# Windowed attention in a fused transformer kernel: probabilities turned on VectorE in 32x32 blocks and placed by DMA instead of turned on TensorE

## The reference, cut to what matters

```
h = layernorm(layernorm(x)) ; qkv = h @ qkv_w + qkv_b         # 16 heads of 16
scores = einsum('bld,blwd->blw', q, kw) / 4                   # each token sees 15 neighbours
attn = softmax(scores, axis=-1)
out = einsum('bld', attn, vw) ; x = x + (shortcut + out @ proj_w + proj_b, then gelu MLP 256-1024-256)
main = gelu(x @ W1m + b1m) @ W2m + b2m
top_vals, top_idx = top_k(softmax(mean(x) @ w_gate + b_gate), 2)
out = x + a * main + (1 - a) * sum_k gate_k * (gelu(x @ W1e[k] + b1e[k]) @ W2e[k] + b2e[k])
```

## Time and profile before

| | |
|---|---|
| Median of 3 runs | 1894.2 us (1894.03 to 1895.52) |
| Profiled execution: span | 1891.2 us |
| PE busy | 1877.7 us (99%) |
| DVE busy | 1348.4 us (71%) |
| ACT busy | 1173.0 us (62%) |
| POOL busy | 875.4 us (46%) |
| DMA | 121.88 MB, mean 64 GB/s |

### The profile page before, as it was taken

The page is one execution under the profiler, slowest core; times in us unless marked ns, Lnnn a source line. Parts: engine busy times, 40 slices in busy tenths (PEclk is TensorE's granted clock), DMA queues, the critical chain, the costliest instruction groups (busy, mean ns, idle before and its releaser), DMA issues.

```text
span 1891.2 us, 49280 instructions
## 1 busy us (share of the span) xinstructions
PE 1877.7 (99%) x19591; PEld 1684.3 (89%) x19591; DVE 1348.4 (71%) x2230; ACT 1173.0 (62%) x1832; POOL 875.4 (46%) x788
## 2 busy tenths in 40 slices
PE   8999999999999999999999999999999999999999
PEld 6889898898988989889898888988889898898998
DVE  7776877777677686776767767677776777777644
ACT  5775755657566575665756657566575655657554
POOL 6555271542715436153362524536245271552725
PEclk9999999999999999999999999999999999999999
DMA  4220312203122031210313113131131311203121
GB/s 141 67 86 28 96 57 54 71 29 96 57 70 64 20 102 51 83 58 24 96 45 90 51 31 94 40 96 47 41 89 34 96 57 48 77 29 96 46 62 57
DMA packets 147437, 121.88 MB, mean 64 GB/s; under 512 B 17964, under 2 KB 140040, under 8 KB 147208
## 3 DMA queue, kind: packets, MB, share of 16 engines
q1 hardware_dynamic: 146512, 117.90, 21.7%
q10 hardware_dynamic: 696, 0.83, 0.2%
HBM read 85.52 MB, written 8.39 MB: 50 GB/s over the span
## 4 chain that ended last, share of the span: by engine, by line
PE 97%; DVE 1%; ACT 0%; DMA 0%; issue 0%; POOL 0%; ACTq 0%; DVEq 0%; POOLq 0%
PE psB L253 58%; PE psA L253 28%; PE psA L1258 3%; PE psA L1275 3%; PE psA L1297 2%; PE psA L1147 2%; PE psA L1313 0%; DMA raw<-in_L_attn_qkv_w 0%; DVE smax L733 0%; POOL wf_lo L501 0%; DVE smax L720 0%; DVE pr L737 0%; DVE hr_lo L622 0%; PE psB L1332 0%; DMA xin<-in_L_attn_x 0%
## 5 line engine op out<-in xcount | busy, mean ns | idle before, releaser
L622 DVE TENSOR_TENSOR hr_lo<-hf,hr_hi 128x512 fp32r<-128x512 f32 x512 | 484.0, 945 | 467.4 <-ACT hr_hi L976 467.4
L510 POOL TENSOR_SCALAR wx_hi<-raw 128x512 fp32r<-128x512 f32 x256 | 201.6, 788 | 668.6 <-DMA raw<-in_L_ffn_W2e 390.4
L976 ACT ACTIVATE hr_hi<-hf 128x512 fp32r<-128x512 f32 x512 | 324.4, 634 | 277.8 <-PE psB L253 189.7
L512 POOL TENSOR_TENSOR wx_lo<-raw,wx_hi 128x512 fp32r<-128x512 f32 x256 | 409.3, 1599 | 21.4
L253 PE MATMUL psB<-wx_hi,hr_hi 128*128 128x256 f32 x1016 | 287.6, 283 | 1.5 <-DVE acc L654 0.3
L972 ACT ACTIVATE hf<-psB,b1x 128x512 f32<-128x512 f32 x256 | 175.3, 685 | 176.1 <-PE psB L253 173.4
L253 PE MATMUL psB<-wx_hi,hr_lo 128*128 128x256 f32 x1016 | 284.2, 280 | 0.0
L253 PE MATMUL psB<-wx_lo,hr_hi 128*128 128x256 f32 x1016 | 283.6, 279 | 0.0
L253 PE MATMUL psB<-z_hi,wx_hi 128*128 128x512 f32 x512 | 212.1, 414 | 0.0
L253 PEld LDWEIGHTS psB<-wx_hi,hr_hi 128*128 128x128 f32 x1016 | 191.0, 188 | 19.6 <-issue 7.3
L253 PE MATMUL psB<-z_hi,wx_lo 128*128 128x512 f32 x512 | 202.4, 395 | 0.0
(11 more groups left out here) (207 smaller groups left out, 4644.0 us busy)
## 6 DMA issues: line engine op xcount, KB each, us to landing
raw<-in_L_ffn_W1e SPq DMA_DIRECT2D x256, 128.0 KB, 2.3
raw<-in_L_ffn_W2e SPq DMA_DIRECT2D x256, 128.0 KB, 2.2
vb<-vs SPq DMA_DIRECT2D x64, 192.0 KB
vb<-vs SPq DMA_DIRECT2D x64, 160.0 KB
out_x<-acc SPq DMA_DIRECT2D x31, 256.0 KB, 2.2
xin<-in_L_attn_x SPq DMA_DIRECT2D x15, 512.0 KB, 3.8
tm<-in_L_ffn_b2e SPq DMA_DIRECT2D x32, 128.0 KB, 3.3
raw<-in_L_attn_fc_w SPq DMA_DIRECT2D x8, 256.0 KB, 3.1
```

Of the source, the lines that this page charges most:

```text
L510: g.tensor_scalar(wx[0][:, s, :], raw[:, s, :], 1.0, 0.0, ALU.mult, ALU.add).then_inc(w_hi.sem, 1)
L512: g.tensor_tensor(wx[1][:, s, :], raw[:, s, :], wx[0][:, s, :].bitcast(f32), ALU.subtract).then_inc(w_lo.sem, 1)
L622: v.tensor_tensor(hr[1][:, c % 2, :], hf[:, c % 3, :], hr[0][:, c % 2, :].bitcast(f32), ALU.subtract).then_inc(h_lo.sem, 1)
L976: a.activation(hr[0][:, c % 2, :], hf[:, c % 3, :], ACT.Copy).then_inc(h_hi.sem, 1)
```

## The change

Row 0 stays nearly as it is (`turn_first`, `turned_first`). In rows 1 to 15:

- `turn` on PE and `turned` on ACT go. In their place DVE turns a unit in blocks of 32x32 with one instruction (`turn_blocks`), behind `normalise`: units 0 to 3 at q 3, 4, 8 and 9. The result goes into `y` (unit 0), the new tile `blk` (units 1 and 2) and `sx` (unit 3).
- Such blocks still lie on the wrong partitions. SP places them with 12 transfers of 32 partitions x 1 KB per unit, from SBUF to SBUF (`place_turned`). They stand in SP's list ahead of load 5 (unit 0), load 6 (unit 1) and load 8 (units 2 and 3).
- `attend` of units 0 and 1 both stand at q 8, and of units 2 and 3 both at q 12. Each waits for the 12 transfers of its unit.
- The queries of unit 2 are written by ACT at q 3 (`query_blocks_first`), no longer by DVE.
- `norm1_y` on ACT moves from q 5 to q 6 and waits until unit 0 has been placed, since its output is `y`. On POOL `norm1_bias` moves from q 7 to q 8. The second `attended_low` on DVE moves from q 12 to q 13.
- A unit's two groups stand 48 keys apart instead of 64. Paddings and the memsets of paddings go.

```diff
-    PK = GW + KW
-    HP = 32
+    PK = G * KW
+    SQ = 32
+    PB = PK // SQ
+    UW = UB * PK
+        blk = sb("blk", [P, UW])
+        def turned_flat(t, u):
+            if t == 0:
+                return tokens_flat(sx if u % 2 else pT)
+            return tokens_flat(acc) if u == 1 else pr[:, 0:UB * P] if u == 3 else tokens_flat(pT)
+        def blocks(u):
+            flat = tokens_flat(y)[:, 0:UW] if u == 0 else tokens_flat(sx)[:, 0:UW] if u == 3 else blk[:, :]
+            return flat.rearrange("p (c b k) -> p c b k", c=PB, b=UB)
+        PLACED = {RING + 1: (0,), RING + 2: (1,), 2 * RING: (2, 3)}
+            def place_turned(t, u):
+                sp.wait_ge(blk_s.sem, blk_s.at(t - 1, u))
+                if u == 0:
+                    sp.wait_ge(t1_lo.sem, t1_lo.all(t))
+                    sp.wait_ge(av.sem, av.all(t - 1))
+                elif u == 1 and t > 1:
+                    sp.wait_ge(store.sem, store.all(t - 2))
+                elif u == 2:
+                    sp.wait_ge(av.sem, av.at(t, 1))
+                for s in range(HS):
+                    for c in range(PB):
+                        dst = turned_flat(t, u)[SQ * c:SQ * c + SQ, s * UB * QB:(s + 1) * UB * QB]
+                        src = blocks(u)[SQ * s:SQ * s + SQ, c, :, :].rearrange("p b k -> p (b k)")
+                        sp.dma_start(dst, src).then_inc(pT_in[u].sem, 16)
+                            if t < ROWS and n in PLACED:
+                                for u in PLACED[n]:
+                                    place_turned(t, u)
...
+            def turn_blocks(t, u):
+                v.wait_ge(normed.sem, normed.at(t, u))
+                if u == 0:
+                    v.wait_ge(sx_s.sem, sx_s.at(t - 1))
+                elif u == 1 and t > 1:
+                    v.wait_ge(pT_in[2].sem, pT_in[2].all(t - 2))
+                elif u == 2:
+                    v.wait_ge(pT_in[1].sem, pT_in[1].all(t - 1))
+                elif u == 3:
+                    v.wait_ge(acc_s.sem, acc_s.at(t - 1, 1))
+                src = pr[:, (u % 2) * UW:(u % 2 + 1) * UW].rearrange("p (b c k) -> p c b k", c=PB, k=SQ)
+                v.transpose(blocks(u), src).then_inc(blk_s.sem, 1)
...
             def norm1_y(t):
                 if t:
                     a.wait_ge(sx_s.sem, sx_s.at(t - 1))
+                    a.wait_ge(pT_in[0].sem, pT_in[0].all(t - 1))
...
                     elif q == 3 and t:
                         keys(t, 1)
+                        query_blocks_first(t, 1)
...
             def attend(t, u):
+                if t:
+                    pe.wait_ge(pT_in[u].sem, pT_in[u].all(t - 1))
```

More of the change, by code:

```diff
@@ L237, in build @@
         normed, trp, pT_s, av = signal("normed", 4), signal("trp", 8), signal("pT", 8), signal("av", 8)
+        blk_s, pT_in = signal("blk", 4), [signal(f"pT_in{u}", HS * PB, 16) for u in range(4)]
         tA_hi, tA_lo, proj = signal("tA_hi", KD), signal("tA_lo", KD), signal("proj", 2)
@@ L553, in _ @@
                         weights(8, 12)
-                    elif q == 7 and t:
+                    elif q == 8 and t:
                         norm1_bias(t)
@@ L784, in norm1_z @@
                 v.wait_ge(rstd[0].sem, rstd[0].at(row - 1))
-                v.wait_ge(trp.sem, trp.all(row - 1))
+                if row > 1:
+                    v.wait_ge(av.sem, av.all(row - 1))
+                else:
+                    v.wait_ge(trp.sem, trp.all(0))
                 for i in range(NT):
@@ L907, in _ @@
                         route_bias(f)
-                    elif q == 12 and t < ROWS:
+                    elif q == (13 if t else 12) and t < ROWS:
                         attended_low(t, 1)
@@ L1081, in _ @@
                         else:
+                            turned_first(0)
                             exp(t, 2)
-                    elif q == 5 and t:
+                    elif q == 6 and t:
                         norm1_y(t)
                     elif q == 6:
-                        turned(t, 1)
-                        if t == 0:
-                            exp(t, 3)
-                            norm1_y(t)
+                        turned_first(1)
+                        exp(t, 3)
+                        norm1_y(t)
                     elif q == 7 and t:
@@ L1171, in chunk_up @@
                         pe.wait_ge(t2_lo.sem, t2_lo.at(t, k))
-                    last = three(pe, ps[:, m % 2, :], w1[k], [a[:, k, off:off + T] for a in z], k == 0, k == KD - 1)
+                    last = three(pe, ps[:, m % 2, :], w1[k], [a[:, k, :] for a in z], k == 0, k == KD - 1)
                 last.then_inc(up.sem, 1)
@@ L1212, in project_qk @@
                         pe.wait_ge(t1_lo.sem, t1_lo.at(t, k))
-                    last = three(pe, psA[:, bank, :], [w[:, k, col:col + P] for w in wqkv], [z[:, k, LEFT:LEFT + T] for z in zT], k == 0, k == KD - 1)
+                    last = three(pe, psA[:, bank, :], [w[:, k, col:col + P] for w in wqkv], [z[:, k, :] for z in zT], k == 0, k == KD - 1)
                 last.then_inc(qk.sem, 1)
@@ L1304, in project @@
                         for k in parts:
-                            last = three(pe, proj_bank(t, h)[:, j * D:(j + 1) * D], [z[:, k, LEFT + i * P:LEFT + (i + 1) * P] for z in zT],
+                            last = three(pe, proj_bank(t, h)[:, j * D:(j + 1) * D], [z[:, k, i * P:(i + 1) * P] for z in zT],
                                          [w[:, k, :] for w in wproj], k == 0 and j == 0, k == KD - 1 and j == 1)
@@ L1410, in _ @@
                             attend(t, 0)
-                            turn(t, 2)
+                            turn_first(2)
                     elif q == 8:
+                        if t:
+                            attend(t, 0)
                         attend(t, 1)
-                    elif q == 10:
-                        turn(t, 2 if t else 3)
-                    elif q == 11:
+                    elif q == 10 and t == 0:
+                        turn_first(3)
+                    elif q == 11 and t == 0:
                         attend(t, 2)
+                    elif q == 12:
                         if t:
-                            turn(t, 3)
-                    elif q == 12:
+                            attend(t, 2)
                         attend(t, 3)
```

180 lines of the change are left out of this document (87 added, 93 removed).

## The result

The changed kernel takes 2120.51 us (median of 4 runs, 2119.78 to 2125.75) against 1894.12 us before (4 runs, 1893.31 to 1895.52). The ratio is 1.1204, 95% interval 1.1189 to 1.1219. The prediction had the sign right and the mechanism mostly right, but its 2032 us is 88 us short, and the range, which ended at 2085, does not hold the time. The profiled span grew from 1891.2 to 2119.1 us: 228 us, or 15.2 us in each of 15 rows, where 9.2 were forecast.

The account below looks back on a forecast made before the run. PE, busy 1877.7 of 1891.2 us, was taken as the bound, with SP's transfers making it wait: 15 rows x 9.2 = 138 us on 1891, plus 3, gives 2032 us; own range 1985 to 2075, eight in ten 1945 to 2085.

Parts of the forecast that it names:

- I take 0.544, and 0.04 between two, so 0.58 per transfer: SP's placing DMAs: issue time plus gap, giving 7.0 us per unit and 28 us of SP per row.
- 700.2 + 36d: Row 6: start of chunk 13 with issue time d per transfer; 721.1 for 0.58, against 711.93 before the change.
- Rival 3: PE's clock halves after its waits; swallowed behind the first, 0 to 44 us behind the second; 12% for over 15 us.
- Rival 2: SP's transfers cost the windows' median, 0.78 with gap: +16.3 us per row, 2139 us; range 0.63 to 0.78 gets 7%.
- the chain unit 0, `norm1_y`, chunk 7, chunk 8, `normalise`, blocks of unit 2: ACT and DVE: unit 0's landing at 692.7 delays each following step, so unit 2's blocks are ready at 704.8.
- the transposition: DVE's transposition of 128x768, absent from the trace before: taken as 0.95 us, bounds 0.5 and 2.0.
- where PE waits and how often: PE waits for DMA at `attend`, near 6.5 us for unit 1 and near 5 for unit 3, 15 of each.
- PE's saving: PE without turns and with paired attends: 3.9 us per row, 58 us in all, 1836 us if nothing came late.
- the landing: Placed data reach their destination 1.65 us after SP's last issue has ended, read from row 0's windows.
- the last products: PE's one attend between the last landing at 720.4 and chunk 13 at 721.1: 0.7 us.
- The 0.6 for saved entries: PE: two fewer entries into blocks of small products, 0.1 us gap and 0.1 late start each, added as 0.6 per row.
- rival 4: SP's issues are hidden (under 0.3 us each), PE late only for DVE: 1.4 to 3.9 us saved per row, 1836 to 1873; 8%.

Follow-up runs that it names:

- The run with spare products: Changed kernel plus 30 and 14 unused matmuls per row on PE ahead of its waits for units 1 and 3: 2097.29 us.
- the run with one queue: Changed kernel with one of twelve transfers in each of units 0 and 1, all twelve in units 2 and 3: 2044.66 us.

## Why the prediction was wrong in size

Two terms make most of the 90 us between 138 and 228, and both stood in the prediction as rivals instead of in its sum.

1. **The step that failed first: "I take 0.544, and 0.04 between two, so 0.58 per transfer".** It is 0.67 as a mean over the trace: median 0.59, plus a tail of stretched issues. In the prediction's own formula 700.2 + 36d, d = 0.67 puts chunk 13 at 724.3; measured 724.8 in row 6. That is 3.2 us per row by the formula and 3.7 as measured, 48 to 56 us (some 0.3 of the 3.7 is the clock, in the products of unit 3). The rows had warned: I took the smallest record of the windows as the typical one of a smaller transfer, though the biases' row has a median of 0.556 and a maximum of 1.170. Factors of 36 stand behind this one number.
2. **The clock, counted at nothing in the sum.** Behind the second wait PE needs 4.54 us for a chunk instead of 2.91, 1.6 us in the mean (2.1 in row 6), and 0.3 more for the products of unit 3 in most rows. That is 24 to 28 us in all. Another 0.6 us per row, 9 us, are the slower products of point 6. Rival 3 had the place right and the price within its bounds (half clock, swallowed behind the first wait, 0 to 44 us behind the second) and 12% for over 15 us. It happens in every row. The run with spare products (at least 1.55 per row) and the run with one queue (2.5 per row behind one wait) bear it out.
3. **Rivals that don't exclude each other.** Rival 2's interval (d of 0.63 to 0.78) and rival 3 were given 7 and 12% as if only one could come. Together, d = 0.67 gives 2080, and with 24 to 44 us for the clock 2104 to 2124, which holds the time; the range ended at 2085.
4. **Held:** the chain unit 0, `norm1_y`, chunk 7, chunk 8, `normalise`, blocks of unit 2 (each step within the shift handed on to it); the transposition (0.978 us against 0.95); where PE waits and how often; that PE's saving does not show. PE's wait at unit 1 was 8.3 us where 6.5 was forecast, at unit 3 3.8 where near 5 was. That is again the issue time: the first wait holds all of the first queue's excess, and the slow clock eats into the second.
5. **Held by compensation:** the landing took 1.3 us instead of 1.65, the last products 1.0 instead of 0.7, which is the lower clock again.
6. **Wrong with little effect here:** PE's saving, 3.9 us per row in the forecast, is 2.7. The turns' share of it (3.26) was read rightly, but the changed kernel gives back 1.1 to 1.2 us per row through slower products of 256 columns, which nothing in the forecast foresaw. Of these, 0.6 lie outside the stretch with the waits and reach the time, as 9 us. The 0.6 for saved entries was also more than its own terms give: two entries of 0.2 us are 0.4. And rival 4 had the lateness of DVE's two results at 0.8 and 1.7 us, where PE waits 2.0 and 2.0 in the traced row. The rest lies beneath the transfers' waits in the changed kernel. In rival 4 it all matters: with transfers as good as free the kernel came to 1919 us, slower than before, and not 1836 to 1873. Its balance per row: 2.7 us saved, 3.5 of waits for DVE, and some 1.0 for the clock behind them (an estimate: 9 falls with 3.3 us of work each at half speed), so 1.8 us lost, which is the 27.

Why about one issue in twenty is stretched to 1.1 to 2.0 us stays open. It is so in the kernel before too (the window's maximum is 1.743) and in the reads from HBM (1.760), so it isn't the change's.

## What to carry to other kernels

Work that left the engine which bounds the kernel was paid for in issues here. So count the DMAs that an edit adds, multiply by the median and not by the minimum of the nearest row, add the tail, and ask where in the queue they all have to be through. Where a new wait of several microseconds on TensorE is certain, as the two here were, the half clock behind it belongs into the sum, not among the rivals. Two rivals that can both come true need a chance for both together. Taking away one suspect shows only the next one: the transpositions' 45 us came to light when the transfers were gone, and moving them back brought the landings out again.

## What the runs showed of the hardware

- An issue on SP of 32 KB from SBUF to SBUF (32 partitions, 1 KB each) takes 0.59 us in the median, and SP is held that long; with one end in HBM 0.42 us for 128 KB and 0.34 to 0.38 for 384 KB written.
- Such data land 1.8 to 1.9 us after the issue's start, 1.3 after its end.
- A 32x32 transposition of 128x768 fp32 on VectorE takes 0.978 us, without spread (978 to 981 ns).
- With one transfer per unit, PE was granted 1.2 GHz already behind waits of 2.0 to 2.5 us for VectorE, in 9 of 15 rows, and worked at it for some 3 us. In the other 6 rows waits of the same 2.0 us left it at 2.4 GHz.
- Six turns of 128x112 more in a group cost PE 0.65 us, so 0.11 each. Of 360 left out, 39 us by this, 27.5 us reached the run's time.
- Products of 256 columns at full clock follow each other 118.0 ns apart in the kernel before and 120.5 to 120.9 ns apart in the versions of the changed kernel whose traces were counted. The cause is open.
